# Shared-key attention and a routed expert layer on one core: smaller GpSimd copies, another engine for one DMA, and reordered steps

## The chip, the cores and the metric

The kernel is one program on one core of a Trainium2 chip. The metric is device time in microseconds (us). Three runs of the kernel before gave a median of 484.14 us (478.88 to 484.38). One more execution was profiled: 479.42 us by the same measure, 477.7 us of it the profiler's span. TensorE (PE) multiplies, ScalarE (ACT) applies functions, VectorE (DVE) does elementwise work and reductions, GpSimd (POOL) does copies and the indirect DMAs, and SyncE (SP) only issues DMAs.

## What is computed

The input `x` holds 8 batches of 256 rows with 256 columns, 2048 tokens. Cut to what matters, the reference is

```
xn  = layernorm(x)                                   # over 256 columns
q   = xn Wq' + bq ; k, v = xn Wk' + bk, xn Wv' + bv  # 16 heads of 16; ONE key and value head
s   = q k' / 4, causal ; attn = softmax(s)
att = (attn v) Wout' + bout
top = the 4 largest of softmax(xn Wr') over 16 experts, scaled to sum 1
ffn = sum over the 4 chosen e of top_e * ((silu(xn Wg_e) * (xn Wu_e)) Wd_e)
out = x + att + ffn
```

All arithmetic is fp32. Queries and keys are held as a high part and a remainder, stacked along the contracted partitions, so that one matmul in the fp32r type gives full scores.

## The kernel before, in words

Every engine runs its own instruction list, in the order in which the functions are called in its block. Semaphores join them. The program has three stages.

**Front.** The tokens are worked in four groups of 512 (`g` = 0 to 3). DVE measures mean and variance and forms the scale (`measure`, `scale`, lines 1099 to 1119), ACT writes the normalised rows (`normalise`, line 906), PE transposes them (line 617) and projects to keys, values and router logits (line 647) and queries (line 659), ACT and DVE split each into high part (lines 946, 958) and remainder (lines 1193, 1208). SP stores queries and keys to DRAM (`q_d`, `k_d`, lines 371, 367) and loads them back in the layout that the scores want: keys by `load_k` (line 346), queries by `load_q` (line 351, 8 DMAs per batch, into one of three buffers `qs`). POOL fills constant rows. Partitions 64 to 95 of `qs` hold rows that say which query of a block of 32 a column is; `from_rows(buf)` (line 463) writes them. Together with constant rows of the keys `ks` they add the causal mask inside the matmul.

**Batches.** For each batch there are 12 blocks of scores (`NB`). A block is computed twice. The first pass, `scores_for_max` (line 638), contracts 96 rows, and DVE takes the maximum of each block in `row_max` (line 1188), which allows PE at most two blocks ahead. When the 12 blocks of a batch are done, DVE joins the maxima (`join_max`, line 1278), PE transposes them (`transpose_max`, line 687), and DVE forms the negative maximum of each query as a high part and a remainder (`split_max`, lines 1284 to 1287, semaphore `nm_ready`). Two DMAs write these as rows 96 and 97 of `qs` (`load_m`, line 387, semaphore `m_in`). The second pass, `scores` (line 696), contracts 98 rows, so that ACT can apply the exponential directly (line 979). The first pass runs 18 blocks ahead of the second. In step `s` of batch `b`, PE computes one block of each pass, and then what the step number calls for: the product with the values (`weigh_v`, line 707), the transpose of the context (`context`, line 719), of the divided context (`transpose_context`, line 729) and the output projection (`project_out`, line 735). ACT copies between these (`keep_context`, line 985; `keep_cxt`, line 990), DVE divides (`normalise_context`, lines 1292, 1295) and adds (`add_out`, line 1303). `transpose_context` writes the PSUM bank that also holds the transposed maxima, so it waits for `nm_ready`.

The router works in the shadow of the first batches: `top_logits`, `top_experts`, `shift_tops`, `mark_choices` (line 1165, a one-hot table), `join_choices` (line 1172), `sum_tops`. From batch 2, step 9 on, 16 calls of `list_rows` on PE (line 743), one every second step, collect the token list of each expert tile from tables that POOL (line 543) and DVE (line 1310) write.

**Experts.** 79 tiles of 128 rows: POOL gathers rows with one indirect DMA (line 557), PE, ACT and DVE compute the expert, and POOL adds the result to DRAM with another (line 571).

What the change touches on each engine: on SP the loop over `g` and the calls `load_k(GW, T)` and `load_m(0)` behind it; on POOL `from_rows`, the key copies `copy_k(b)` (line 483, from the loaded keys to `ks`), the additions of the output bias `add_bias(g)` (line 474) and `weigh_choices` (line 512); on PE and ACT one step number each in `batch`; on DVE the front's loop over `g`, and in `batch` the places of `split_max`, `normalise_context` and the router's first marks.

## Time and profile before

| | |
|---|---|
| three runs | 484.14, 478.88, 484.38 us |
| profiled execution | 479.42 us, span 477.7 us |
| PE matmul busy | 410.7 us, 86% of the span |
| POOL busy | 297.5 us, 62% |
| DVE busy | 209.4 us, 44% |
| ACT busy | 187.3 us, 39% |
| front | 0 to 65 us |
| batches | 65 to 191 us |
| experts | 191 us to the end |

Busy shares of a whole span are means over three stages with different limits. What a step costs is read from the stage in which it lies: from the timelines of two engines side by side, where one shows an idle gap ("[1.65 <-ACT early L906]": idle 1.65 us until that instruction of ACT ended), and from the chain of work that ended last.

### The profile page before, as it was taken

To read this page: it belongs to the slowest core of one execution; us is meant where nothing else is said; L and a number is where in the kernel's file an instruction comes from. 1 tells how busy PE (TensorE), PEld (TensorE's weight loads), DVE (VectorE), ACT (ScalarE), POOL (GpSimd) and SP (SyncE) were. 2 spreads that over 40 slices of the span, in tenths; PEclk is the share of its full clock that TensorE was granted. 3 is DMA by queue.
4 is the path that set the end of the run, shared out by engine and by line. 5 is a ranking of instruction groups with operands and counts; after the bars stand their busy time and mean duration, and the time that the engine had idled before them with its cause. 6 is when DMAs were issued, how large, how long until landed. Compare 5 with 4: busy or idle time off the path is not lost.

```text
span 477.7 us, 6790 instructions
## 1 busy us (share of the span) xinstructions
PE 410.7 (86%) x1687; PEld 226.5 (47%) x1688; DVE 209.4 (44%) x514; ACT 187.3 (39%) x439; POOL 297.5 (62%) x304
## 2 busy tenths in 40 slices
PE   3998779788989797889999999999999999999920
PEld 1342334445545343456655555555555555545510
DVE  5778877887886652122223223322222322323300
ACT  4483134456675555323333323333333333323300
POOL 7955331059992021148788788788788788888740
PEclk9998658999999999899999999999999999999985
DMA  7289935987699456525455545445444544446126
GB/s 240 89 204 240 263 106 134 192 176 132 169 251 162 136 150 208 165 60 88 71 82 88 75 72 87 71 82 83 73 79 81 80 79 82 79 73 84 24 36 140
DMA packets 54034, 57.17 MB, mean 120 GB/s; under 512 B 11376, under 2 KB 48928, under 8 KB 53760
## 3 DMA queue, kind: packets, MB, share of 16 engines
q0 software_dynamic: 15440, 21.51, 27.4%
q1 hardware_dynamic: 25904, 22.87, 21.1%
q10 hardware_dynamic: 12672, 12.58, 8.9%
q8 instruction: 7, 0.11, 0.1%
q14 instruction: 11, 0.09, 0.1%
HBM read 37.40 MB, written 23.33 MB: 127 GB/s over the span
## 4 chain that ended last, share of the span: by engine, by line
PE 44%; issue 14%; POOL 11%; DMA 10%; DVE 8%; SPq 5%; ACT 4%; ACTq 0%; POOLq 0%; DVEq 0%
PE bank L830 15%; PE bank L846 8%; POOL late L557 6%; DMA late<-xn_d,get_row 4%; PE bank L707 4%; PE bank L735 3%; PE bank L696 3%; PE bank L638 3%; PE bank L820 3%; POOL out_dram L571 2%; DVE pmax L1188 2%; POOL odd_d L571 2%; SPq L351 2%; PE bank L838 2%; DMA qs_wgu<-nm 1%
## 5 line engine op out<-in xcount | busy, mean ns | idle before, releaser
L830 PE MATMUL bank<-wgu,late 128*128 x316 | 151.6, 602 | 3.0 <-issue 1.2
L557 POOL DMA_INDIRECT late<-xn_d,get_row x79 | 83.5, 1056 | 72.3 <-PE bank L696 28.7
L1399 DVE SCALAR_TENSOR_TENSOR late<-late,bank 128x256 f32<-128x256 f32 x79 | 37.9, 480 | 156.7 <-ACT late L1055 156.7
L846 PE MATMUL bank<-wdn,late 128*128 x316 | 81.5, 380 | 1.4 <-DVE late L1406 1.4
L1055 ACT ACTIVATE late<-bank 128x256 f32<-128x256 f32 x79 | 30.4, 385 | 129.7 <-PE bank L830 129.7
L979 ACT ACTIVATE pt<-bank 128x512 f32<-128x512 f32 x96 | 56.0, 599 | 62.8 <-PE bank L696 61.7
L1188 DVE TRANSPOSE_TENSOR_REDUCE pmax<-bank 128x16 f32<-128x512 f32 x96 | 66.3, 705 | 24.8 <-PE bank L638 24.3
L830 PEld LDWEIGHTS bank<-wgu,late 128*128 128x128 f32 x316 | 53.7, 190 | 46.1 <-issue 45.4
L571 POOL DMA_INDIRECT out_dram<-late,slots x40 | 63.6, 1589 | 19.0 <-issue 9.5
L571 POOL DMA_INDIRECT odd_d<-late,slots x39 | 61.9, 1588 | 12.8 <-issue 9.8
L846 PEld LDWEIGHTS bank<-wdn,late 128*128 128x128 f32 x316 | 53.9, 190 | 6.5 <-issue 2.4
L1406 DVE COPY late<-bank 128x256 f32<-128x256 f32 x79 | 33.5, 424 | 32.4 <-PE bank L838 32.3
L820 PEld LDWEIGHTS bank<-ident,late 128*128 128x128 f32 x158 | 19.5, 140 | 56.2 <-DMA late<-xn_d,get_row 44.2
L1066 ACT ACTIVATE late<-bank 128x256 f32<-128x256 f32 x79 | 30.4, 384 | 39.2 <-PE bank L846 39.2
L543 POOL TENSOR_SCALAR wgu<-iota_p,slot_pf 128x128 f16<-128x128 f32 x64 | 38.7, 625 | 0.3
L820 PE MATMUL bank<-ident,late 128*128 128x128 f32 x158 | 31.7, 282 | 6.1 <-DMA late<-xn_d,get_row 5.8
L638 PE MATMUL bank<-qs_late,ks 96*128 96x512 f32 x60 | 31.9, 542 | 4.5 <-DVE pmax L1188 4.3
L1059 ACT ACTIVATE late<-bank 128x256 f32<-128x256 f32 x79 | 30.0, 380 | 6.9 <-PE bank L820 6.6
L838 PE MATMUL bank<-ident,late 128*128 128x128 f32 x158 | 30.2, 273 | 0.0
L707 PE MATMUL bank<-pt,v_all 128*32 128x512 f32 x192 | 27.3, 642 | 0.0
L838 PEld LDWEIGHTS bank<-ident,late 128*128 128x128 f32 x158 | 22.2, 141 | 7.9
L483 POOL CAST ks<-wdn 64x640 fp32r<-64x640 f32 (+1 forms) x16 | 11.0, 713 | 23.7 <-PE bank L696 16.0
(143 smaller groups left out, 402.2 us busy)
## 6 DMA issues: line engine op xcount, KB each, us to landing
qs_late<-q_d SPq DMA_DIRECT2D x40, 128.0 KB, 4.7
q_d<-early SPq DMA_DIRECT2D x16, 256.0 KB, 4.6
wgu<-in_L_ffn_w_gate_dram ACTq DMA_DIRECT2D x8, 512.0 KB, 5.2
wgu<-in_L_ffn_w_up_dram ACTq DMA_DIRECT2D x8, 512.0 KB, 4.6
wdn<-in_L_ffn_w_down_dram ACTq DMA_DIRECT2D x8, 512.0 KB, 4.3
qs_wgu<-q_d SPq DMA_DIRECT2D x24, 128.0 KB, 4.5
xs<-in_L_attn_x_dram SPq DMA_DIRECT2D x4, 512.0 KB, 4.0
xn_d<-early SPq DMA_DIRECT2D x4, 512.0 KB, 4.3
```

What stands on the lines that cost most here:

```text
L543: pool.tensor_scalar(hot_p[:, t % HOTS, c], iota_p[:], slot_pf[:, t, c:c + 1], None, ALU.is_equal).then_inc(hot_p_ready, 1)
L557: pool.indirect_dma_start(xg[:, j % RING, :], None, xn_d, bass.IndirectOffsetOnAxis(ap=get_row[:, j:j + 1], axis=0), bounds_check=last_row ...
L571: pool.indirect_dma_start(odd_d if j % 2 else out_rows, bass.IndirectOffsetOnAxis(ap=slots[:, j:j + 1], axis=0), ys[:, j % RING, :], None, ...
L638: pe.matmul(bank[:, N % 2, :], k, q, start=True, stop=True).then_inc(p1_ps, 1)
L707: mm = pe.matmul(bank[32 * j:32 * j + 32, 5, :], v_all[:, 2 * b + kt, :], weights[:, j], start=(kt == 0), stop=(g != 1), skip_group_check= ...
L820: t = pe.transpose(bank[:, 7, c * P:(c + 1) * P], xg[:, r, c * P:(c + 1) * P], ident[:, :])
L830: mm = pe.matmul(bank[:, 2 + buf, :], xT[:, buf, c, :], wgu[:, bass.ds(e * KC + c, 1), :], start=(c == 0), stop=(c == KC - 1))
L838: t = pe.transpose(bank[:, 6, c * P:(c + 1) * P], hh[:, buf, c * P:(c + 1) * P], ident[:, :])
L846: mm = pe.matmul(bank[:, 4 + buf, 0:D], hT[:, buf, c, :], wdn[:, bass.ds(e * FC + c, 1), :], start=(c == 0), stop=(c == FC - 1))
L979: act.activation(pt[:, G % 2, n % NU, :], bank[:, 3 + N % 2, :], ACT.Exp).then_inc(exp_done, 1)
L1188: dve.tensor_reduce(found, bank[:, N % 2, :].rearrange("p (h q) -> p h q", h=H), AX.X, ALU.max, apply_transpose=True).then_inc(max_done, 1)
L1399: dve.scalar_tensor_tensor(out=hh[:, buf, :], in0=hh[:, buf, :], scalar=xg[:, r, bass.ds(e + D, 1)], in1=bank[:, 2 + buf, F:2 * F], op0=AL ...
```

## The change

Nothing of the arithmetic is changed. The parts are:

1. `from_rows` writes each half of a buffer in four copies of 512 elements, not in one of 2048. The counts in the waits on `qs_padded` follow.
2. On ACT, behind the copy of the output weights, two DMAs write the first batch's maxima. SP's `load_m(0)` is gone.
3. Keys are loaded in three parts: a second part (`load_k(GW, 2 * GW)`) stands in SP's loop at `g == 2`, the rest comes where it came before. `copy_k(2)` and `copy_k(3)` wait for the second part only. POOL does all `add_bias` and `copy_k(2)` ahead of `weigh_choices(0)`.
4. `mark_choices(0)` and `join_choices(0)` move from DVE's front loop to steps 4 and 5 of batch 0. `split_max(0)` moves ahead of `sum_tops(0)`.
5. In each batch, `context(b - 1, 1)` on PE moves from step 3 to step 4, behind `project_out(b - 1, 0)`. `normalise_context(b - 1, 1)` on DVE moves from step 5 to step 6, and `keep_cxt(b - 1, 1)` on ACT from step 10 to step 9.
6. `split_max(b + 1)` moves within DVE's step 8 ahead of the step's `row_max`.

```diff
@@ SP @@
                 if g == 0:
                     load_k(0, GW)
+                if g == 2:
+                    load_k(GW, 2 * GW)
                 if g < 3:
...
-            load_k(GW, T)
+            load_k(2 * GW, T)
 
             for g in range(2, NG):
                 sp.wait_ge(q_stored[g], 64)
-            load_m(0)
@@ POOL @@
             def from_rows(buf):
                 for half in range(2):
-                    pool.tensor_copy(qs[buf][64:96, half].rearrange("p h (u q) -> p (h u) q", q=QC),
-                                     from_q[64:96].unsqueeze(1).to_broadcast([32, H * NU, QC])).then_inc(qs_padded, 1)
+                    for h in range(0, H, H // 4):
+                        pool.tensor_copy(qs[buf][64:96, half, h:h + H // 4].rearrange("p h (u q) -> p (h u) q", q=QC),
+                                         from_q[64:96].unsqueeze(1).to_broadcast([32, H // 4 * NU, QC])).then_inc(qs_padded, 1)
...
-                pool.wait_ge(k_all_in, 64 if b < 2 else 128)
+                pool.wait_ge(k_all_in, 64 if b < 2 else 128 if b < 4 else 192)
...
             shift_logits(0)
-            add_bias(1)
-            weigh_choices(0)
-            for g in range(2, NG):
+            for g in range(1, NG):
                 add_bias(g)
-            pool.wait_ge(coef_ready, 1)
             pool.wait_ge(xb_ready, NT)
             copy_k(2)
             pool.wait_ge(k_ready, 6)
+            weigh_choices(0)
             shift_logits(1)
@@ PE, batch @@
                         if s == 3:
+                            project_out(b - 1, 0)
+                        if s == 4:
                             context(b - 1, 1)
-                            project_out(b - 1, 0)
@@ ACT @@
             act.activation(woT[:].rearrange("p c e -> p (c e)"), bank[:, 6, :], ACT.Copy).then_inc(w_act, 1)
+            act.wait_ge(nm_ready, 1)
+            for a in range(2):
+                act.dma_start(qs[0][96 + a:97 + a].rearrange("o e h t -> o (e h t)").bitcast(F32),
+                              nm[:, a, :].bitcast(F32)).then_inc(m_in[0], 16)
...
-                        if s == 10:
+                        if s == 9:
                             keep_cxt(b - 1, 1)
@@ DVE @@
                 if g == 2:
-                    mark_choices(0)
-                    join_choices(0)
                     row_max(0, 0)
...
+                if (b, s) == (0, 4):
+                    mark_choices(0)
+                if (b, s) == (0, 5):
+                    join_choices(0)
...
+                    if s == 8 and b < B - 1:
+                        split_max(b + 1)
                     n = b * NB + s + NB + NB // 2
                     if n < B * NB:
                         row_max(n // NB, n % NB)
...
-                        if s == 5:
+                        if s == 6:
                             normalise_context(b - 1, 1)
...
-                    if s == 8 and b < B - 1:
-                        split_max(b + 1)
...
             join_max(0)
+            split_max(0)
             sum_tops(0)
-            split_max(0)
```

How DVE's order moves in the front, from the third group's query remainders on. Before (`chosen` and `wgu` are the router's tables, `pmax` the block maxima):

```order
L1208 SCALAR_TENSOR_TENSOR early<-bank,bq_s,early 128x512 x2
L1165 TENSOR_TENSOR wgu<-top_ef,iota_e 128x512
L1172 TENSOR_REDUCE chosen<-wgu 128x128
L1188 TENSOR_REDUCE pmax<-bank 128x16
L1193 SCALAR_TENSOR_TENSOR early<-bank,bvrk,early 16x512
```

and now:

```order
L1213 SCALAR_TENSOR_TENSOR early<-bank,bq_s,early 128x512 x2
L1193 TENSOR_REDUCE pmax<-bank 128x16
L1198 SCALAR_TENSOR_TENSOR early<-bank,bvrk,early 16x512
L1193 TENSOR_REDUCE pmax<-bank 128x16
L1213 SCALAR_TENSOR_TENSOR early<-bank,bq_s,early 128x512
```

The two router instructions no longer stand ahead of the first block maximum; they come in batch 0.

How PE's order moves in steps 3 and 4 of a batch (here batch 1). Before, step 3 begins at the first row:

```order
L638 MATMUL bank<-qs_late,ks 128x512
L696 MATMUL bank<-qs_late,ks 128x512
L719 MATMUL bank<-ident,ct 128x128 x4
L735 MATMUL bank<-woT,out_buf 128x256 x2
L638 MATMUL bank<-qs_late,ks 128x512
L696 MATMUL bank<-qs_late,ks 128x512
```

and now:

```order
L638 MATMUL bank<-qs_late,ks 128x512
L696 MATMUL bank<-qs_late,ks 128x512
L735 MATMUL bank<-woT,out_buf 128x256 x2
L638 MATMUL bank<-qs_late,ks 128x512
L696 MATMUL bank<-qs_late,ks 128x512
L719 MATMUL bank<-ident,ct 128x128 x4
```

The context transpose, which waits for ACT's copy `ct`, comes one projection and one pair of score blocks later.

SP's issues of groups 2 and 3, before:

```order
L371 DMA q_d<-early 128x4x128 x4
L351 DMA qs_late<-q_d 16x2x1024 x8
L367 DMA k_d<-early 16x512 x2
L371 DMA q_d<-early 128x4x128 x4
L346 DMA wdn<-k_d 16x1536 x4
L387 DMA qs_wgu<-nm 1x128x32 x2
```

and now:

```order
L371 DMA q_d<-early 128x4x128 x4
L346 DMA wdn<-k_d 16x512 x4
L351 DMA qs_late<-q_d 16x2x1024 x8
L367 DMA k_d<-early 16x512 x2
L371 DMA q_d<-early 128x4x128 x4
L346 DMA wdn<-k_d 16x1024 x4
```

Four issues more stand in this run, and the first maxima are no longer at its end.

## Rows read from the trace of the kernel before

**Rows 1.** The page: PE's granted clock in tenths, in 40 slices of 11.94 us.
```profile
PEclk9998658999999999899999999999999999999985
```

**Rows 2.** Busy time by stretch: us, PE (x) PEld (x) DVE (x) ACT (x) POOL (x), clock, DMA share, GB/s.
```profile
131.00:147.00 16.00, 14.26 (x93) 8.38 (x93) 13.00 (x29) 10.66 (x23) 15.16 (x24) 1.00 0.96 231
...
265.00:340.00 75.00, 72.48 (x277) 42.36 (x276) 20.81 (x46) 24.66 (x69) 60.94 (x47) 1.00 0.48 79
```

**Rows 3.** DVE's timeline, front: start, duration, engine, line, operation, [idle before <-releaser].
```profile
18.64 1.52 DVE L1114 TENSOR_TENSOR rstd<-rstd,var_e 128x4 f32<-128x4 f32 x1
...
22.39 1.58 DVE L1118 SCALAR_TENSOR_TENSOR shift<-mv,rstd 128x4 f32<-128x4 f32 x1
...
29.09 0.16 DVE L1114 TENSOR_TENSOR rstd<-rstd,var_e 128x4 f32<-128x4 f32 x1
```

**Rows 4.** POOL's timeline, front: a copy of 512 elements, and the copies of 2048.
```profile
14.20 0.61 POOL L456 CAST ks<-after_q 32x512 fp32r<-32x512 f32 x1
...
16.42 3.72 POOL L463 CAST qs_wgu<-from_q 32x2048 fp32r<-32x2048 f32 x2
```

**Rows 5.** Timelines of ACT and PE, front, third group.
```profile
24.00 2.08 ACT L906 ACTIVATE early<-xs,shift,rstd 128x256 f32<-128x256 f32 x4 [2.26 <-DVE shift L1118]
...
24.66 1.92 PE L617 MATMUL bank<-ident,early 128*128 128x128 f32 x8 [1.65 <-ACT early L906]
```

**Rows 6.** DVE's timeline, front, around the first block maximum.
```profile
40.05 0.75 DVE L1165 TENSOR_TENSOR wgu<-top_ef,iota_e 128x512 bf16<-128x512 f32 x1
40.83 1.04 DVE L1172 TENSOR_REDUCE chosen<-wgu 128x128 bf16<-128x512 bf16 x1
41.79 0.71 DVE L1188 TRANSPOSE_TENSOR_REDUCE pmax<-bank 128x16 f32<-128x512 f32 x1
```

**Rows 7.** PE's timeline, front, last group's query projections.
```profile
39.55 1.95 PE L659 MATMUL bank<-early,wqT 128*128 128x512 f32 x4
42.55 0.50 PE L638 MATMUL bank<-qs_wgu,ks 96*128 96x512 f32 x1 [1.04 <-DVE pmax L1188]
...
44.42 3.42 PE L659 MATMUL bank<-early,wqT 128*128 128x512 f32 x4
```

**Rows 8.** The chain that ended last, 56 to 65 us: start, duration, what.
```profile
56.56 5.17 DMA q_d<-early
...
62.80 2.15 DMA qs_wgu<-nm
```

**Rows 9.** Timelines of DVE and PE: first maxima, first block of the second pass.
```profile
56.99 0.66 DVE L1287 TENSOR_TENSOR nm<-nm_f,nm 128x32 fp32r<-128x32 f32 x1
...
61.69 0.76 PE L638 MATMUL bank<-qs_late,ks 96*128 96x512 f32 x1 [0.36 <-DVE pmax L1188]
64.99 0.80 PE L696 MATMUL bank<-qs_wgu,ks 98*128 98x512 f32 x1 [2.53 <-DMA qs_wgu<-nm]
```

**Rows 10.** SP's timeline: the four loads of the last keys.
```profile
59.15 1.71 SPq L346 DMA_DIRECT2D wdn<-k_d  x4
```

**Rows 11.** The chain that ended last, later: the slowest transfer of maxima.
```profile
158.04 4.86 DMA qs_wgu<-nm
```

**Rows 12.** Waits of PE, 82 to 195 us: total us, times, longest us.
```profile
PE bank L719 <- ACT ct L985: 4.7, 7, 1.0
PE bank L735 <- ACT out_buf L990: 3.9, 8, 0.7
PE bank L729 <- issue: 3.2, 5, 1.3
```

**Rows 13.** DVE's timeline, batch 4: after step 3's wait, and the maxima's last instruction.
```profile
136.16 0.72 DVE L1188 TRANSPOSE_TENSOR_REDUCE pmax<-bank 128x16 f32<-128x512 f32 x1 [1.46 <-PE bank L638]
...
141.81 0.32 DVE L1287 TENSOR_TENSOR nm<-nm_f,nm 128x32 fp32r<-128x32 f32 x1
```

**Rows 14.** Timelines of POOL and PE: list tables, and a list matmul.
```profile
132.51 12.22 POOL L543 TENSOR_SCALAR wgu<-iota_p,slot_pf 128x128 f16<-128x128 f32 x20
...
149.75 0.32 PE L743 MATMUL bank<-wgu 128*128 128x80 f16 x4
```

More of the change, by code:

```diff
@@ L462, in from_rows @@
                 for half in range(2):
-                    pool.tensor_copy(qs[buf][64:96, half].rearrange("p h (u q) -> p (h u) q", q=QC),
-                                     from_q[64:96].unsqueeze(1).to_broadcast([32, H * NU, QC])).then_inc(qs_padded, 1)
+                    for h in range(0, H, H // 4):
+                        pool.tensor_copy(qs[buf][64:96, half, h:h + H // 4].rearrange("p h (u q) -> p (h u) q", q=QC),
+                                         from_q[64:96].unsqueeze(1).to_broadcast([32, H // 4 * NU, QC])).then_inc(qs_padded, 1)
             from_rows(0)
-            pool.wait_ge(qs_padded, 2)
+            pool.wait_ge(qs_padded, 8)
             def add_bias(g):
@@ L486, in _ @@
             from_rows(1)
-            pool.wait_ge(qs_padded, 4)
+            pool.wait_ge(qs_padded, 16)
             add_bias(0)
@@ L492, in _ @@
             from_rows(2)
-            pool.wait_ge(qs_padded, 6)
+            pool.wait_ge(qs_padded, 24)
             copy_k(1)
@@ L633, in scores_for_max @@
                     pe.wait_ge(q_in[b % 3][n // NU], 64 * (b // 3 + 1))
-                    pe.wait_ge(qs_padded, 2 * (b % 3) + n // NU + 1)
+                    pe.wait_ge(qs_padded, 8 * (b % 3) + 4 * (n // NU) + 4)
                 if N >= 2:
```

## The prediction

> **What bounds the kernel now.** I read three views in this order: busy time by stretch, the chain of waits that ended last, and the timelines of PE, DVE, ACT, POOL and SP side by side where the chain changes engine. The first tells the stages apart. In the expert stage PE is busy 72.48 of 75 us with POOL at 60.94 [rows 2]. The change touches nothing there, so I leave that stage, more than half of the span, as it is. In a middle batch (16 us) PE is busy 14.26 us and DVE 13.00 [rows 2]: neither is full, they hand blocks back and forth, and each batch loses time in named gaps. In the front the chain runs through DVE, ACT and PE to the fourth group, then through SP's issues and a DMA to the first block of the second pass.
>
> **The front.** (a) *Quarter copies.* DVE's `scale(2)` has two instructions of 1.52 and 1.58 us at 18.64 and 22.39; the same first one in the next group takes 0.16 [rows 3]. POOL's copies of 2048 elements, 1.86 us each, run back to back from 16.42 and go on for a second buffer [rows 4], and the slow instructions end when a copy ends: 16.42 + 3.72 = 20.14 against 18.64 + 1.52 = 20.16. So DVE waits there for a whole copy, three times (a third, between these two, is of their length). A copy of 512 takes 0.61 us [rows 4], so a wait is at most that and about 0.4 on average: three waits cost 1.2 us, not the roughly 4.3 of now. `scale(2)` ends some 3.2 us earlier, near 20.7. But ACT has other work until 21.75 (24.00 less its idle 2.26), so ACT gains 2.25, and PE, which was idle 1.65 for the first row tile and then followed ACT tile by tile [rows 5], gains about 2.2. Everything behind it in groups 1 and 2 is a chain of ACT, PE and DVE without slack and moves by 2.2. POOL pays four starts for one: 4 x 0.61 = 2.44 against 1.86, 0.6 for each half and 3.5 for six. It has that time, since it sits idle for keys around 27 to 32 us and again for 13 us later.
>
> The Trainium skill (SBUF — State Buffer, section "Who interferes with whom") says that a DVE instruction with two inputs in SBUF and a GpSimd instruction that reads SBUF exclude each other for a whole instruction, the first to issue going first. The trace agrees in the 1.52 us of [rows 3]. If POOL, always first, kept DVE out for a whole run of quarters, DVE would wait for 16 x 0.61 = 9.8 us from 16.42, to 26.2, and lose 2 us where I count 3.2 gained; I take the other reading because DVE's instructions got in between two copies (the slow one above ended with the second copy, and others followed before the third ended).
>
> (b) *Router marks.* DVE did the one-hot and its sum, 0.75 and 1.04 us, right ahead of the first `row_max` [rows 6], for which PE stood idle 1.04 [rows 7]. Without them that maximum is 1.8 us earlier still, but the next one waits for ACT's keys, so the fourth group gains about 1.4 more, 3.6 in all. There is a second effect. PE's projection of the last half took 3.42 us where the same four matmuls took 1.95 before it [rows 7]: the granted clock had gone to 1.2 GHz after two idle gaps. With one of them gone and the other at 0.7 I expect it to still be at 2.4 GHz there, 1.5 us more: 5.1. Bounds: 3.6 and 5.1. Then eight `row_max` follow at DVE's pace, unchanged, so the first maxima, ready at 57.65 now [rows 9], are ready near 52.6. In batch 0 the marks cost DVE 1.8 us again, between steps 4 and 6, where it sits idle about 2 us for PE: nothing. Swapping `split_max(0)` and `sum_tops(0)` (0.4 us) is no gain, since the sums stood in the shadow of a transpose; it pushes the six maxima of batch 1 back by 0.4.
>
> (c) *The first maxima's DMA.* It now leaves behind the last query store, which landed at 61.73, and itself takes 2.15 from its second issue at 62.80 [rows 8]. PE could have begun batch 0 at about 62.2 but waited until 64.99 [rows 9]. Issued by ACT, which has nothing queued behind it before batch 0 needs these rows, it leaves at 52.7, with the second issue at 53.3. It then runs beside SP's transfers. Its duration is not in the trace for this place: 2.15 is the quiet value [rows 8], 4.86 the one with a crowd of other transfers [rows 11]. I take 4.5, as the queues are full there: 57.8. PE's side is ready at 62.2 - 5.1 + 0.4 = 57.5. So batch 0 begins near 57.9, **7.1 us earlier**. With a low clock in (b) it is 58.9 and 6.1; with a DMA of 2.15 nothing is added, since PE is the later one.
>
> The Trainium skill (DMA: Bandwidth & Descriptors, section "Queues, rings and completion order") says that each DMA engine takes turns between the queues it has work for. By that the maxima would not stand behind SP's backlog and would need nearer 2.15 than 4.86. The sum would gain only 0.3.
>
> (d) *Keys in three parts.* Four more issues on SP, 4 x 0.43 = 1.7 us [rows 10], stand ahead of the queries of batch 2 and of the last stores. SP is continuously busy there from 24.66 on; it now starts 3.2 earlier with (a), so the last query store lands 1.5 earlier, not later, and nobody waits for it but the first expert load. `copy_k(2)` was ready at 64.7 for a use at 72; now it is ready near 52. Worth nothing by itself, but needed: its slack of 7 us would be what (c) takes.
>
> **The batches.** Between 82 and 195 us PE waits 4.7 us in seven places for the copy `ct` ahead of `context(b-1, 1)`, 3.9 in eight for the copy ahead of `project_out`, and 3.2 in five ahead of `transpose_context(b-1, 1)`, which is held by `nm_ready` [rows 12].
> - The first goes: with the projection and a pair of blocks (0.9 + 0.6 us) ahead of it, `ct` is long there. 4.7.
> - The second: `keep_cxt` at step 9 follows its transpose at once, no longer behind an exponential. Seven of the eight are this one: 3.4.
> - The third: DVE's chain in batch 4 from 136.16, after 1.46 us idle, to 142.13 is nearly unbroken [rows 13]. Its start moves with PE's block of step 4, which comes 1.0 earlier (0.5 of wait and 0.5 of transposes go behind it), and `split_max` no longer has a `row_max` of 0.65 ahead of it. PE's wait of 0.54 goes. 3.2 in all.
>
> Together 11.3. What is late next is the maxima's DMA: in batches 5 and 6 PE already waits for it at the start of the next batch, with 4.86 us [rows 11], and there only the earlier `nm_ready` counts, 1.1 and 0.7. That leaves 0.9 of the 11.3 on the path: **10.4**. Batch 0 to 1, where PE waits for the same DMA, gains 0.65 from `split_max`: **0.7**.
>
> Not covered: POOL. It writes list tables without a pause, 0.61 us each, 20 in 12.22 us [rows 14]; the last of 64 is ready at 144.7 and used at 149.75 [rows 14]. That lead of 5.0 us shrinks by the 4.5 that three batches gain; the tables behind a `copy_k` have 4.0. I take 0.6 back.
>
> Sum: 7.1 + 0.7 + 10.4 - 0.6 = 17.6. Against the profiled execution, 479.42 - 17.6 = **461.8**. That execution is 4.7 below the median of the three runs and 0.5 above the lowest; the same gain from 484.14 gives 466.5. I give 464 for a median of runs that may fall at either.
>
> **The rivals.**
> 1. *Only the front gains.* DVE and PE are coupled over two blocks; `row_max` of step 8 now follows `split_max`, and DVE, busy 13 of 16 us, may hand back at steps 9 to 11 what was won. For: both engines are above 80%. Against: after step 9 DVE shows idle gaps of about 1 us for PE. Gain 7.8, time 471.6 to 476.3.
> 2. *Only the batches gain,* because the front ends in something else (the port, the DMA of maxima, the queries of batch 1 from a full SP). With 2 to 4 of the 7.1 left: gain 12.5 to 14, time 465 to 471.
> 3. *The clock, slower.* The clock is low from about 45 to 75 us [rows 1] and costs little, as DVE sets the pace. If DVE's added 1.8 us in batch 0 and the shifted handoffs leave PE too broken up, it stays low in batches 1 to 5. Four matmuls take 3.42 for 1.95 then [rows 7], so 14.26 us of PE work would be some 22 to 24 in a batch of 16: 6 to 8 us lost for each. It decides from the fourth such batch: 462 + 4 x 7 = 490, and to 500. Against: with the gaps shorter, PE is busier.
> 4. *Nothing.* Both parts turn into waits of the same size: 479 to 484.
>
> **How the numbers follow.** Forecast 0.66, rival 1 0.13, rival 2 0.14, rival 3 0.02, rival 4 0.05. From 484.14, 2% is 9.7 us, about what a measurement of this kernel can tell from no change: 474.5. The forecast and rival 2 are faster (0.80), with a third of rival 1 (0.04); the rest of rival 1 (0.09) and rival 4 (0.05) are within 2% (0.14); rival 3 is slower (0.02). The range: the forecast's bounds are 461.8 less 2 where parts add (a quick DMA, a batch 0 at 2.4 GHz) and less 2 for a low run, 458, and 466.5 with a low clock in (b) and twice the loss to POOL, 469. To take in rival 2 and the lower half of rival 1 it reaches to 474.5.
>
> **What the next profile would show.** Right: DVE's instructions of `scale(2)` under 0.8 us; PE's second projection of group 3 near 1.95 us; the first second-pass block near 58 us; no wait of PE for `ct`; batches of about 14.6 us, not 16.2; tiles as before. Wrong: the projection at 3.4 us; PE waiting for a `row_max` at steps 9 to 11 by 0.5 us or more a batch; list matmuls waiting for POOL by over 1 us in all; a maxima DMA of over 6 us.

## The result, and the profile after

The changed kernel took 468.09 us (median of four runs, 464.84 to 472.9) against 482.29 us (478.88 to 484.38) before: ratio 0.9701, interval 0.9648 to 0.9755. Timed again (the last run below) it gave 0.9694 (0.9638 to 0.9750). The forecast's range of 458 to 474.5 holds the median, which lies 4 us above the 464. The ratios leave out executions more than 1.5% above the fastest of their kernel, such as the 472.9 here and the profiled 470.96 of the last run below. The gain of 14.2 us between medians is less than the 17.6 us that the prediction summed, and between the two profiled executions it is 9.4: 479.42 to 470.03, span 477.7 to 468.3.

Where did it come from? Busy time by stretch shows it (us, PE (x) PEld (x) DVE (x) ACT (x) POOL (x), granted clock, DMA share, GB/s). The cuts are the first block of the second pass and the first expert matmul. Before:

```profile
0.00:65.00 65.00, 46.23 (x127) 19.73 (x128) 47.90 (x139) 27.54 (x55) 40.59 (x68) 0.87 0.78 202
65.00:196.07 131.07, 112.99 (x606) 60.11 (x606) 89.31 (x214) 73.91 (x147) 51.55 (x81) 0.95 0.72 173
...
```

After:

```profile
0.00:61.87 61.87, 45.11 (x127) 19.07 (x128) 44.96 (x137) 27.55 (x55) 42.34 (x86) 0.87 0.85 201
61.87:186.97 125.10, 112.26 (x605) 60.56 (x606) 91.37 (x216) 74.63 (x147) 51.36 (x81) 0.94 0.77 182
...
```

The front gives 3.1 us where 7.1 were forecast, the batches 6.0 where 10.5 were (0.7 + 10.4 - 0.6), and the rest of the span 0.3 (281.6 to 281.3). The engines' busy times in the whole span are nearly the same (PE 410.7 and 410.5 us); what went is waiting.

**The batches.** The waits of PE from 60 to 190 us (line, who released it: total us, times, longest us) answer to [rows 12]:

```profile
PE bank L696 <- DMA qs_late<-nm: 5.2, 3, 2.0
PE bank L696 <- DMA qs_wgu<-nm: 4.1, 2, 2.8
PE bank L638 <- DVE pmax L1193: 1.6, 5, 0.3
...
PE bank L719 <- DVE out_buf L1298: 0.7, 1, 0.7
PE bank L729 <- issue: 0.7, 1, 0.7
...
PE bank L735 <- ACT out_buf L995: 0.5, 1, 0.5
```

The three waits that the change aims at summed to 11.8 and sum to 1.9. In their place stand the first two lines: PE waits for the DMA that brings the next batch's maxima. Less the 2.8 at batch 0 it is 6.6 us, at the start of batches 2, 5, 6 and 7. The DMAs did take longer (min/median/max from issue to landing of all of SP's `load_m`, in the kernel before with batch 0's among them), before and then after:

```profile
DMA to landing us min/median/max: 2.0/2.8/4.9
```

```profile
DMA to landing us min/median/max: 2.0/4.3/5.5
```

**The front.** DVE's timeline answers to [rows 3], the chain of waits to [rows 8], with ACT, PE and POOL around the fourth group between them (start, duration, line, operation, [idle before <-releaser]):

```profile
19.21 0.54 DVE L1119 TENSOR_TENSOR rstd<-rstd,var_e 128x4 f32<-128x4 f32 x1
19.79 0.52 DVE L1120 TENSOR_TENSOR rstd<-rstd,std 128x4 f32<-128x4 f32 x1
20.34 0.54 DVE L1121 TENSOR_SCALAR rstd<-rstd 128x4 f32<-128x4 f32 x1
```

```profile
30.73 1.26 POOL L485 CAST ks<-wdn 64x640 fp32r<-64x640 f32 x2 [2.44 <-DMA wdn<-k_d]
32.06 4.51 POOL L465 CAST qs_late<-from_q 32x512 fp32r<-32x512 f32 x8
36.64 1.27 POOL L485 CAST ks<-wdn 64x640 fp32r<-64x640 f32 x2
37.99 0.41 POOL L507 TENSOR_TENSOR logits<-logits,top_w 128x128 f32<-128x128 f32 x1
```

```profile
38.43 0.31 ACT L918 ACTIVATE probs<-logits 128x128 f32<-128x128 f32 x1 [1.17 <-POOL logits L507]
```

```profile
41.59 0.50 PE L638 MATMUL bank<-qs_wgu,ks 96*128 96x512 f32 x1 [1.78 <-DVE pmax L1193]
41.93 2.76 PE L659 MATMUL bank<-early,wqT 128*128 128x512 f32 x4
```

```profile
53.80 0.20 DVE nm L1290
...
54.02 0.55 ACTq L976
...
54.62 7.21 DMA qs_wgu<-nm
...
61.87 0.80 PE bank L696
```

The quarters did what was expected of them: the three slow instructions of `scale(2)` take 0.54 us or less each. Then POOL is late. Its copies for buffer 2 take 4.51 us for 3.73, they stand between two key copies and the shift of the router's logits, and the keys came late, at 30.7 us, where most runs below with the same front have them at 29.0 to 29.6.

That lateness begins at 12 us, in the second group's `scale`. DVE's third instruction there took 1.15 us and ended with a constant fill on POOL (12.36 + 1.05 = 13.41). In e5 below it took 0.17:

```profile
12.29 1.15 DVE L1121 TENSOR_SCALAR rstd<-rstd 128x4 f32<-128x4 f32 x1
```

```profile
12.36 1.05 POOL L459 MEMSET ks<- 32x1152 f32 x1
```

```profile
12.30 0.17 DVE L1121 TENSOR_SCALAR rstd<-rstd 128x4 f32<-128x4 f32 x1
```

The long form is in five of the fourteen profiled executions: this one, e7, e8, e11 and e12. In these, DVE begins the third group's `scale` at 19.2 us and not at 18.3 to 18.6. In four of them, all but e7 with its whole copies, SP stores the third group's queries from 22.2 and POOL waits 1.9 to 2.5 us for the keys; the other executions with quarters have 21.0 to 21.6 and 0.6 to 1.3. No part of the change touches this place. So a time in the front is best compared between executions that begin alike.

Back at the fourth group, ACT waits 1.17 us for the logits, PE 1.78 for a maximum, and the last projection takes 2.76 us, part of it at 1.2 GHz. The maxima are ready at 54.0, not near 52.6, and their DMA takes 7.2 us, not 4.5.

### The profile page after: what moved, and what is told of

The parts are those of the page before. It is cut to its first block, busy times and chain, and to the rows that moved or that the text cites. A ratio compares the mean times of both kernels' runs of the same rounds, so it can differ in the third digit from the quotient of the medians.

```text
span 468.3 us, 6811 instructions
## 1 busy us (share of the span) xinstructions
PE 410.5 (88%) x1687; PEld 226.4 (48%) x1688; DVE 208.6 (45%) x514; ACT 187.9 (40%) x439; POOL 298.9 (64%) x322
## 4 chain that ended last, share of the span: by engine, by line
PE 37%; issue 18%; POOL 18%; DMA 11%; DVE 8%; ACT 3%; SPq 2%; ACTq 0%; POOLq 0%; DVEq 0%
PE bank L831 11%; POOL late L557 10%; PE bank L847 5%; PE bank L707 5%; PE bank L638 4%; PE bank L696 4%; POOL odd_d L571 4%; DVE pmax L1193 3%; DMA qs_late<-nm 3%; POOL out_dram L571 3%; DMA qs_wgu<-nm 3%; DMA late<-xn_d,get_row 2%; PE bank L735 2%; PE bank L821 2%; DMA out_dram<-late,slots 1%
## 5 line engine op out<-in xcount | busy, mean ns | idle before, releaser
L821 PEld LDWEIGHTS bank<-ident,late 128*128 128x128 f32 x158 | 19.2, 140 | 54.2 <-DMA late<-xn_d,get_row 43.1
L696 PE MATMUL bank<-qs_late,ks 98*128 98x512 f32 x60 | 24.8, 425 | 5.7 <-DMA qs_late<-nm 5.2
L485 POOL CAST ks<-wdn 64x640 fp32r<-64x640 f32 (+1 forms) x16 | 10.4, 675 | 25.0 <-PE bank L696 14.8
```

The source lines that it names most:

```text
L696: pe.matmul(bank[:, 3 + N % 2, :], k, q, start=True, stop=True).then_inc(s_ps, 1)
L821: t = pe.transpose(bank[:, 7, c * P:(c + 1) * P], xg[:, r, c * P:(c + 1) * P], ident[:, :])
```

## The experiments

"Batch 0" is the start of the first block of the second pass, "the stretch" the time from there to the first expert matmul: 64.99 and 131.08 before, 61.87 and 125.10 after.

**e1_front_only: parts 1 to 4.** The edit takes parts 5 and 6 back:

```diff
                         if s == 3:
+                            context(b - 1, 1)
                             project_out(b - 1, 0)
-                        if s == 4:
-                            context(b - 1, 1)
```

(and likewise for `keep_cxt`, `normalise_context`, `split_max`.)

> Parts 1 to 4 of the change alone (quarter copies, first maxima's DMA on ACT, keys in three parts, router marks in batch 0); the batches' step numbers and the place of split_max as before. Theory A (the transfers of a batch are what bounds it after the change, so the two halves of the change do not add in full): batch 0 begins near 61.9 us as in the changed kernel, 3.1 earlier than before, and the stretch from there to the first expert matmul takes 130 to 131 us as before (64.99 to 196.07), since batches of 16.2 us leave the DMA engines time to drain. Span about 474.5, ratio near 0.994. Theory B (the front's gain is partly lost in the batches by DVE's two marks): that stretch is longer, 132 to 133 us, and nothing or 1 us is left of the gain.

Measured: 473.18 us, ratio 0.9843 (0.9753 to 0.9933). Batch 0 at 58.91, the stretch 131.08, as before to the hundredth. PE's waits in the batches are back, and those for the maxima are short:

```profile
PE bank L719 <- ACT ct L989: 4.7, 7, 1.0
PE bank L729 <- issue: 3.2, 5, 1.3
PE bank L735 <- ACT out_buf L994: 2.7, 6, 0.7
...
PE bank L696 <- DMA qs_late<-nm: 1.4, 2, 1.1
```

The front alone gives 6.1 us at batch 0 and keeps it. It is the same front as in the changed kernel, whose batch 0 began at 61.87 in its profile. Here DVE's early instruction was short, the keys were in time, ACT waited 0.47 us for the logits and the projection took 1.88.

**e2_batches_only: parts 5 and 6.** The kernel before with those edits.

> Parts 5 and 6 alone (context to step 4, normalise to step 6, keep_cxt to step 9, split_max ahead of row_max). Theory A: batch 0 begins at 65.0 us as before; PE's waits ahead of L719, L729 and L735 between batches 1 and 7 fall by about 10 us, and 4 to 5 us come back as waits for the maxima's DMA, so the stretch to the first expert matmul is 125 to 126 us instead of 131.1. Gain 5 to 6, ratio near 0.988. Theory B (the batches' lost gain comes of the shifted front, by another phase of the transfers): the stretch is 121 us, gain 10, ratio 0.979.

Measured: 473.75 us, ratio 0.9826 (0.9720 to 0.9932). Batch 0 at 66.03, the stretch 124.96. So the batches' parts give 6.1 us by themselves, with the old front: what is missing of the forecast 10.5 is lost inside the batches and needs no new front. The product of the two ratios is 0.967, that of the whole change 0.970: within the intervals the halves add. Each alone is a gain of under 2%, but both intervals end below 1.

**e3_first_m_on_sp: the first maxima's DMA back on SP,** behind the last query stores.

```diff
-            act.wait_ge(nm_ready, 1)
-            for a in range(2):
-                act.dma_start(qs[0][96 + a:97 + a]...
...
                 sp.wait_ge(q_stored[g], 64)
+            load_m(0)
```

> The changed kernel with the first maxima's DMA again on SP, behind the last query stores and the third part of the keys. Theory A (the 7.2 us of this DMA on ACT are SP's backlog on the 16 DMA engines, and it would be served no sooner from SP): SP issues it at about 64 us, it lands in 2.2 us in empty queues, PE begins batch 0 near 67 us, 5 us later than with ACT; of these 5, 0 to 4 come back later, as the span is bounded by transfers in the batches. Theory B (a DMA from ACT is slow by itself, as the first of its queue): from SP it takes 2.2 us all the same; this run alone does not part the two, the next one does.

Measured: 479.39 us (one run). The chain of waits:

```profile
55.42 6.65 DMA q_d<-early
62.15 0.57 SPq L389
...
62.76 2.18 DMA qs_wgu<-nm
...
64.98 0.79 PE bank L697
```

The maxima were ready near 51.2 and stood for 11 us behind the stores. Batch 0 begins at 64.98, where it began before. All else that the front gains arrives only through this one move. The batches gained nothing here either: the stretch is 131.04, with parts 5 and 6 in place. PE waits 9.9 us in it for maxima, 5.25 of them at batch 2, where one DMA took 8.4 us and the granted clock fell to 1.2 GHz (0.50 from 100 to 106 us). Why that batch met so much isn't known, so the whole 11 us between this run and the others are not the price of the move.

**e4_keys_in_two: part 3's extra load undone,** to see whether the four key issues on SP make the maxima's DMA slow.

```diff
-                if g == 2:
-                    load_k(GW, 2 * GW)
...
-            load_k(2 * GW, T)
+            load_k(GW, T)
```

> The changed kernel without the second part of the keys in SP's loop (keys in two parts, as before); all else as changed. SP spent 4.5 us on these four issues at 46.15 us. Theory A (backlog): the queries of batch 2 and the last stores leave 3 to 4.5 us earlier, the backlog that the first maxima meet at 54.6 us is shorter by as much, the DMA lands in 3 to 4 us instead of 7.2, and PE begins batch 0 near 59 us, where its own six blocks end. Theory B (slow by itself, as the first DMA of ACT's queue): it still takes about 7 us, batch 0 begins near 61.9. In both copy_k(2) ends near 62, before its use in step 6.

Measured: 465.37 us (one run), batch 0 at 58.35, the DMA 5.6 to 6.1 us. That misses the 3 to 4 expected of fewer issues: SP's eight query loads then took 6.38 us to issue for 3.68 and SP came out only about 1 us earlier than in the changed kernel. So this run doesn't tell bytes from issues; e9 does.

**e5_stores_late and e6_stores_weights_late: less for the maxima to meet in the batches.** The first issues two stores (logits, 128 KB, and zeros, 2 MB) in batch 5; the second also shifts four loads of expert weights.

```diff
-                if b == 0:
+                if b == 5:
                     sp.wait_ge(coef_ready, 2)
...
-                if b == 3:
+                if b == 5:
                     zeros = zero_t[:].rearrange("p t e -> p (t e)")
@@ e6 only @@
-                    if b == 5 and s in (7, 9):
-                        load_experts(4, s // 9)
+                    if b == 5 and s in (10, 11):
+                        load_experts(4, s - 10)
...
-                    if b == B - 2 and s in (5, 7):
-                        load_experts(B - 2 + s // 7, 2)
+                    if b == B - 2 and s in (9, 11):
+                        load_experts(B - 2 + s // 11, 2)
```

> The changed kernel with two SP transfers moved out of the batches that are full: the store of the routing weights (128 KB in 64-byte pieces, 10.7 us to landing in batch 1) and the 2 MB of zeros (14 us, batch 4) both go behind the maxima of batch 6, where no more queries are loaded. Theory A (a batch's transfers must drain before its maxima's DMA can land, and shorter batches ran into that): PE's waits for the maxima at the start of batches 2 and 5 (1.7 and 2.1 us) go to under 0.5, those at batches 6 and 7 (1.4, 1.5) stay or grow by 1 as the zeros now pass there; batches 0 to 5 take 76 us and not 79.3. Theory B (the maxima's DMA is slowed by the query loads and weights alone): the two waits stay above 1.2.

Measured: 469.92 us (one run), batch 0 at 57.89, the stretch 129.2. The wait at batch 5 went, with the zeros. But batch 2 waited 3.26 us though the logits' store was gone, and batch 7 3.50, behind zeros that now leave at 150 us. The granted clock fell behind both waits (0.78 from 94 to 100 us, 0.65 from 166 to 174). The stretch is 4.1 us longer than the changed kernel's, where less was expected.

> As the last, and the expert weights that were issued right ahead of the maxima in batches 5 and 6 (steps 7, 9 and 5, 7) go behind them (steps 10, 11 and 9, 11). Theory A: the waits at batches 6 and 7 fall to under 0.7 as well; from batch 0 to the first expert matmul 120 to 121 us, not 125.1, which is the 10.4 us that the prediction summed for the batches. Span 4 us under the changed kernel's at equal front, ratio to the kernel before 0.962 to 0.966. Theory B: 124 us or more, or the first expert matmul waits for the last weights.

Measured: 462.12 us (460.6 to 469.5), ratio 0.9598 (0.9505 to 0.9692). The stretch is 120.03, a gain of 11.0 where the prediction had 10.5. Waits of PE from 60 to 182 us, and the maxima's DMAs:

```profile
PE bank L696 <- DMA qs_late<-nm: 3.3, 3, 2.1
...
PE bank L719 <- DVE out_buf L1298: 0.7, 1, 0.7
PE bank L729 <- issue: 0.7, 1, 0.7
...
PE bank L696 <- DMA qs_wgu<-nm: 0.2, 1, 0.2
```

```profile
DMA to landing us min/median/max: 2.1/2.9/3.7
```

The forecast size of the batches' gain is there, and the maxima's DMAs are back at 2.9 us in the median. The median alone doesn't carry it, though: it is 2.7 in e5 and 3.1 in e2, with stretches of 129.2 and 124.96. What differs is the sum of PE's waits for maxima behind batch 0 (3.4 us here, 8.0 in e5, 4.4 in e2) and the clock, which here is 1.00 from 82 us to the end of the stretch. e5 and e6 run the same program up to batch 5 and yet their waits at batch 2 are 3.26 and 0.21 us: what a DMA of maxima meets varies between executions. And from batch 5 on e6 needs 43.9 us, as e7, e8 and e9 do with the stores in their old places (44.2, 43.9, 43.5): what e6 has over e7 and e8 lies in batches 0 to 4, and there it runs the same program as e5, which needs 3.8 us more. How much of e6's gain is owed to the moved transfers isn't settled.

**e7_whole_copies: part 1 undone.**

```diff
-                    for h in range(0, H, H // 4):
-                        pool.tensor_copy(qs[buf][64:96, half, h:h + H // 4]...
+                    pool.tensor_copy(qs[buf][64:96, half].rearrange("p h (u q) -> p (h u) q", q=QC),
```

> The changed kernel with the constant rows again in copies of 2048 elements. If the prediction's first step is right, two or three of DVE's instructions of the scale wait 1.5 us or more again, the fourth group's first block maximum comes 1.5 to 2.5 us later than in the changed kernel (38.1 us), and SP's first query store too (24 to 25 us, not 22.2). Batch 0 then begins 1.5 to 2.5 us later than with quarters in an execution whose last projection runs at the same clock (58.9 at 2.4 GHz, 61.9 at 1.2), so at 60.5 to 64. If the copies did not matter: no difference in either.

Measured: 467.99 us (one run), batch 0 at 62.11. DVE's timeline, as [rows 3]:

```profile
19.21 0.94 DVE L1118 TENSOR_TENSOR rstd<-rstd,var_e 128x4 f32<-128x4 f32 x1
...
20.38 1.80 DVE L1120 TENSOR_SCALAR rstd<-rstd 128x4 f32<-128x4 f32 x1
...
22.43 1.57 DVE L1122 SCALAR_TENSOR_TENSOR shift<-mv,rstd 128x4 f32<-128x4 f32 x1
```

The changed kernel's profile is the run to set beside it, since DVE begins `scale(2)` at 19.21 in both. `scale(2)` ends at 24.00 and not at 21.54, and PE begins the third group's query projection at 26.45 and not at 23.98: 2.5 us, where the prediction said 2.2. More followed from it. PE, idle 2.07 us before the third group, took 5.29 us for eight matmuls that take 3.60 there:

```profile
24.70 1.92 PE L616 MATMUL bank<-ident,early 128*128 128x128 f32 x8 [2.07 <-ACT early L906]
26.45 5.29 PE L658 MATMUL bank<-early,wqT 128*128 128x512 f32 x8
```

The fourth group's first block maximum comes 3.1 us later (41.25 for 38.11). The first maxima are ready only 1.2 us later (55.2 for 54.0), and batch 0 begins 0.2 later, because the changed kernel's last projection ran partly at 1.2 GHz and this one took 1.88. So the copies' 2.5 us are shown in the third group, and not at batch 0.

**e8_marks_front: the router's marks back ahead of the first `row_max`.**

```diff
                 if g == 2:
+                    mark_choices(0)
+                    join_choices(0)
                     row_max(0, 0)
```

> The changed kernel with the router's two marks again in the front, ahead of the first block maximum. If the prediction's second step is right: that maximum is at 40 us, PE waits for it by 0.7 to 1.1 us and once more for the next, and the last projection takes 2.7 to 3.4 us (it took 1.88 in three of four executions with the marks moved, 2.76 in one). The first maxima are ready 1 to 3 us later than the 51.5 of those three, and batch 0 begins at 60 to 62. Rival: the next block maximum waits for ACT's keys anyway, so the marks cost nothing, the projection takes 1.88 and batch 0 begins at 59.

Measured: 467.39 us (one run), batch 0 at 62.04, the maxima issued at 54.3, 2.9 later than e5's. But this is an execution with DVE's long instruction at 12.3 us, and e5 is not. e11 below is one too, and its DVE reaches the place of the marks at the same time (36.35 there, 36.33 here) with no marks in it. Against e11 the first block maximum is done 1.7 us later (40.10 for 38.39), the second 0.6 later (41.62 for 41.02), since in e11 DVE stands idle 1.14 us for ACT's keys between the two, and the first maxima are ready 2.5 later (54.3 for 51.8). The last projection took 3.01 us, not 1.88: 1.1 of the 2.5 is its clock. Against e12, where the logits are late, the second maximum is no later at all (41.62 for 41.61). So the marks cost 0 to 0.6 us here, and 1.1 by the clock behind them.

**e9_queries_later: the bytes ahead of the first maxima.** SP loads the third batch's queries only once the first maxima are ready.

```diff
-                    if g == 0 or g == 2:
+                    if g == 0:
                         sp.wait_ge(q_stored[g // 2], 64)
-                    for half in range(2):
-                        load_q(g, half)
+                    if g < 2:
+                        for half in range(2):
+                            load_q(g, half)
...
                 sp.wait_ge(q_stored[g], 64)
+            sp.wait_ge(nm_ready, 1)
+            for half in range(2):
+                load_q(2, half)
```

> The changed kernel, but SP loads the third batch's queries (8 DMAs of 128 KB, 8 us of transfer) only once the first maxima are ready, behind the last query stores; ScalarE still issues those maxima. Theory A (backlog): the maxima's DMA took 5 to 7 us in the front because the DMA engines had the bytes of these queries in hand. Without them it lands 2.2 to 4 us behind its second issue, PE is then the later one, and batch 0 begins 0.5 to 1.5 us earlier than in the run with the late stores (57.9), near 57. The queries are first needed near 66 us by PE's first pass, and land near 61 to 63: no wait. Whole time 1 us less than with them early, 464 to 468. Theory B (the issuing queue: a DMA from ScalarE into these rows is slow by itself): it still takes 5 us or more, and nothing moves. Theory C: PE's first pass of batch 2 waits for the late queries, or the second batch's maxima are now late instead; batch 1 or 2 loses 1 to 3 us.

Measured: 464.45 us (one run), batch 0 at 55.73. DMAs issued from 50 to 62 us (KB each, median us to landing), here and then in e10, which has the queries in their old place:

```profile
qs_wgu<-nm ACTq DMA_DIRECT2D x2, 16.0 KB, 2.4
```

```profile
qs_wgu<-nm ACTq DMA_DIRECT2D x2, 16.0 KB, 6.2
```

That is backlog, shown: the same two DMAs from the same engine take 2.4 us instead of 6.2 once 1 MB of query loads stands behind them, and PE no longer waits for them. Theory C holds too. PE waits 1.28 us for the late queries, and 2.09 at batch 1 for that batch's maxima, whose DMA takes 5.56. Batch 1 begins at 74.42, against 73.45 in e5, though batch 0 began 2.2 earlier: the backlog only moved by one batch.

**e10_split_behind_max: part 6 alone undone.**

```diff
-                    if s == 8 and b < B - 1:
-                        split_max(b + 1)
                     n = b * NB + s + NB + NB // 2
...
+                    if s == 8 and b < B - 1:
+                        split_max(b + 1)
```

> The changed kernel, but DVE's split_max of the next batch stands again at the end of step 8, behind that step's row_max. This takes back part 6 alone. Theory A (the prediction's third term): PE's waits ahead of transpose_context(b-1, 1) come back in part, 0.3 to 0.6 us in four or five batches, and the maxima's DMAs leave 0.7 us later, which lengthens the waits for them in batches 2, 5, 6 and 7 (6.6 us in sum now) by 0.5 each; whole time 2.5 to 4.5 us more than the changed kernel. Rival B: the transposes at step 9 are late enough by themselves since other waits went, and only the maxima's waits grow: 1 to 2 us. Rival C: row_max of step 8 comes 1.1 us earlier for PE, which pays back what the maxima lose: no difference over 1 us.

Measured: 467.61 us (one run), batch 0 at 58.66, the stretch 125.93, 0.8 more than with part 6. The transposes' wait is back:

```profile
PE bank L729 <- issue: 3.4, 5, 1.3
```

It was 0.7 with part 6. So part 6 removes 2.7 us of one wait, as Theory A has it, but the time is that of rival C: the batches are 0.8 us longer without it, and executions with the same batches differ by more (125.1 in the changed kernel, 122.9 and 122.2 in e7 and e8). The maxima's waits in the batches are 6.6 us with and without it. What part 6 is worth in time stays open, between nothing and these 2.7 us.

**e11_all_late: e6, e4 and e9 together.**

> All that the runs pointed to, together: the two stores and the expert weights issued later (which gave 462.12 us, ratio 0.9598), keys in two parts, and the third batch's queries issued behind the first maxima. Theory A (these add, since each is about what stands in the DMA engines when a maxima's DMA leaves): batch 0 begins near 57, stretch of the batches 120 us, time 459 to 462, ratio 0.953 to 0.960. Rival B: with the stores gone the backlog at the first maxima is all that is left and PE is already the later one there, so nothing is added: 461 to 463. Rival C: copy_k(2) gets its keys later again and the queries of batch 2 come late, so batch 0 or 1 loses 1 to 3 us: 463 to 466.

Measured: 461.68 us (461.04 to 462.86), ratio 0.9624 (0.9562 to 0.9687), the same as e6. Batch 0 begins at 56.72, the stretch is 121.57. The 0.9 us won at the start went in batch 1. Rival C had named a loss there, but by late keys and queries; this one has another cause. PE's timeline:

```profile
81.96 0.63 PE L721 MATMUL bank<-ident,ct 128*128 128x128 f32 x4 [0.74 <-DVE out_buf L1300]
82.49 0.50 PE L640 MATMUL bank<-qs_wgu,ks 96*128 96x512 f32 x1
82.83 0.40 PE L698 MATMUL bank<-qs_late,ks 98*128 98x512 f32 x1
83.94 0.66 PE L731 MATMUL bank<-ident,out_buf 128*128 128x128 f32 x2 [0.71 <-issue]
84.53 1.94 PE L709 MATMUL bank<-pt,v_all 128*32 128x512 f32 x8
```

After two idle gaps of 0.7 us the granted clock fell to 1.2 GHz (0.63 in the mean from 82 to 88 us), and eight matmuls took 1.94 us. The same eight behind the same two gaps took 1.06 in e6, and batch 1 15.6 us there against 17.9 here.

**e12_changed_again: the changed kernel, timed again.**

> The changed kernel once more, nothing edited, in five rounds. Two questions. Where does batch 0 begin in another execution? Theory A: at 57.6 to 58.9, as in the five runs that share its front, with PE's second projection near 1.9 us and no wait of ScalarE over 0.5 us for POOL's logits; 61.87 was one execution in which the keys' loads came late. Rival B: near 62 again, so the late logits belong to this kernel, and the later stores of other variants cured them. Is it slower than the kernels with the later stores and weights (0.960 and 0.962 of the kernel before)? Theory A: ratio 0.968 to 0.974, its batches 124 to 127 us against 120 to 122, and the two to five us lie in waits for the maxima's DMAs. Rival B: ratio 0.960 to 0.965, and those kernels gained nothing.

Measured: 468.37 us (463.3 to 470.96), ratio 0.9694 (0.9638 to 0.9750). Batch 0 at 59.96, between the two answers: POOL waited 2.52 us for the keys and ACT 1.25 for the logits, as in the first profile, but the projection took 1.88, with PE idle 1.79 before it. DVE's instruction at 12.3 us took 1.15 here too. So late logits belong to this kernel in the executions that begin so, and a low clock behind them in some of those. Against e6 and e11 theory A fits, with ratios of 0.969 and 0.970 on one side and 0.960 and 0.962 on the other, but the intervals overlap: that these two are the better kernels is likely, and not shown.

## Why the prediction was right, point by point

**Right, and why.** The forecast rested on two independent gains, and each came alone: 6.1 us from the front (e1) and 6.1 from the batches (e2). Rival 1 falls with that, and so does rival 4. Rival 3 falls in its size, but not in its kind: the granted clock is 1.00 from 76 us on but for one fall (0.80 from 142 to 150 us), of which more below. (By its own factor, 3.42 for 1.95, its 22 to 24 us for a batch should have been 25.) Rival 2 had a part of it: in the profiled execution the front does end in the DMA of maxima and gives 3.1 us, within its 2 to 4. But e1 and e5 show 6.1 and 7.1 from the same front and e12 5.0, so 3.1 is one execution's price, and rival 2 had the batches give all they were forecast, which they did not.

**(a) Quarter copies, 2.2 us.** Right: 2.5 by e7 at the third group's query projection, and no instruction of `scale(2)` over 0.54 us. The reading that DVE gets in between two quarters holds: three instructions took 0.54, 0.52 and 0.54 us while POOL ran sixteen quarters in a row. By the Trainium skill (SBUF — State Buffer, section "Who interferes with whom") the first to issue holds the port for one instruction; the trace agrees, and DVE did not have to wait for the end of POOL's run.

"POOL has that time" was wrong in the profiled execution. POOL's idle time lies ahead of the key copies, and the added 0.8 us for buffer 2 lies behind them, on the way to the router's logits, for which ACT now arrives 2 us earlier. ACT's wait was 1.17 us, of which the longer copies are 0.8 at most; the late keys are the rest. With the clock behind it the maxima were ready at 54.0, and in e1 and e5 at 51.4 and 51.3. That step was not in the sum. Nor was another, of the other sign: ahead of the first maxima DVE's last two instructions took 0.43 and 0.66 us before, while POOL ran additions from 56.20 on, and 0.18 and 0.19 now that part 3 has moved those forward. That is 0.7 us, and part of why the maxima of e1 and e5 come 6.3 us earlier where 5.1 were summed.

**(b) Marks, 1.4 us and 1.5 of clock.** The clock's part was right in kind: the projection took 3.01 us with the marks (e8), and with this front 1.88 in nine executions and 2.76 in the first profiled one; that is 1.1 of the 1.5. The marks' own part was 0.6 by e11 and nothing by e12, since the next block maximum waited for ACT's keys. No run has the marks in an execution with early keys, so the 1.4 stays open there. In batch 0 the marks cost nothing: it took 15.7 us, 16.1 before.

**(c) The first maxima's DMA, 4.5 us.** The step was right in kind, as e3 shows, and its term mis-sized: 5.4 to 7.2 us from the second issue with the queries in flight. The bound of 4.86 was taken from a batch with a DMA share of 0.45 (158 to 163 us); here the share is 1.08 (54.6 to 61.8). In the executions where the maxima were early (issued at 51.4 to 51.6) this ate what (a) and (b) had won beyond the forecast, and batch 0 began at 57.6 to 58.9, beside the forecast 57.9. With the late logits it was 61.87 and 59.96. By the Trainium skill (DMA: Bandwidth & Descriptors, section "Queues, rings and completion order") the engines take turns between queues, so that ACT's DMA would have needed nearer 2.15. No run agrees while the queries are in flight (5.4 to 7.2); without them it took 2.4 (e9) and 4.0 (e11).

**(d) Keys in three parts, nothing.** Nearly right: `copy_k(2)` ran at 54.1, not 52, and without the early part nothing was lost (e4). The issues took 4.50 us, not 1.7. SP's third group began 2.4 us earlier, as (a) has it for ACT, and not 3.2, and the last query stores were issued from 55.37, 0.4 later than before and not 1.5 earlier.

**The batches, 10.4 us.** The waits went nearly as forecast: the three lines fell by 9.9 us, 11.8 to 1.9, where 11.3 was summed. The step that failed is "what is late next": the prediction kept 0.9 us on the path for the maxima's DMA, with its duration as before. The waits for it behind batch 0 grew from 1.9 to 6.6 us, by 4.7, where the sum had 0.9 more and, at batch 1, 0.7 less. These 4.5 us are the size of what is missing between 10.5 and 6.0. The 1.4 that the three lines fell short is about made up by the 0.6 of the lists and by PE's waits for block maxima (2.8 to 1.6 us). Why the DMAs are late is in part argued: a shorter batch has to move the same bytes, the DMA share rose from 0.72 to 0.77 and the median landing from 2.8 to 4.3 us, and e9 shows the backlog for one batch; but e6, which moves bytes away, differs from e5 by 3.8 us where the two run the same program.

Waits are not all of it. e7 and e8 run the changed kernel's batches, PE waits 6.2 and 5.4 us there for maxima, and their stretches are 122.9 and 122.2 us, gains of 8.2 and 8.9 where the changed kernel's profile has 6.0. The clock goes with the difference, here in the changed kernel and then in e7:

```profile
142.00:150.00 8.00, 8.00 (x45) 4.14 (x45) 3.91 (x7) 4.54 (x9) 0.59 (x2) 0.80 0.71 128
```

```profile
142.00:150.00 8.00, 8.00 (x48) 4.46 (x45) 5.23 (x11) 5.56 (x12) 0.21 (x1) 1.00 0.81 124
```

Both waited 2.0 us for maxima at 141 us; in one the clock fell, in the other it didn't. Before, in e7 and in e8 it is 1.00 from 82 to 180 us; in e2 it falls twice (0.76 from 94 to 100, 0.67 from 142 to 150). So the new waits cost more than their own length in some executions. That is rival 3's mechanism in small, by these stretches 2 to 3 us for one fall, and no run parts it from the waits.

**The lists, -0.6.** Not seen: no wait for the tables appears in the waits after.

**The total.** 464 came nearer than its profiled terms because the median of before lay above its profiled execution, while that of after lay below. The size of each half was forecast as 7 and 10.5 and came as 6 and 6 in e1 and e2; in the changed kernel's first profile the front gave 3.1 of it. That 464 lies so near is in part luck of this kind; that both halves gain is not.

## What to carry to other kernels

Before a part is priced by taking it back, see that the two executions begin alike: here one DVE instruction at 12 us, 1 us longer in five of fourteen executions, moved the front by 0.6 to 1.2 us. When waits are taken out of a loop, price again every transfer that the loop starts: its bytes stay, its time shrinks, and a small DMA that was on time queues behind them. Moving a DMA to an idle engine's queue saves the issue order, not the backlog; for that, bytes must be issued later, and one must look where they then land. A cover named as "the engine is idle there" has to lie behind the added work and ahead of its next reader, not merely near it.

## What was not expected of the hardware

- The four loads of the last keys, 96 KB each, cost SP 1.71 us to issue [rows 10], and four of 32 KB cost 4.50 at 46 us in the changed kernel (3.49 in e1, 5.05 in e5). The DMA share was 1.16 at the quick ones and 1.08 at the slow ones, so full DMA engines alone don't explain it; the cause is open.
- Two idle gaps of 0.7 us were followed by a fall to 1.2 GHz in e11 and not in e6; 1.79 us idle left the projection at 1.88 us in e12, 1.78 at 2.76 in the profiled one. Equal gaps give unequal clocks, and such a step is worth 0.9 to 2.3 us.
- The quarters moved DVE's waits in part: in the next group `scale` now meets POOL's additions, with 0.65 us for instructions that took 0.16:

```profile
26.98 0.65 DVE L1120 TENSOR_TENSOR rstd<-rstd,std 128x4 f32<-128x4 f32 x1
27.67 0.66 DVE L1121 TENSOR_SCALAR rstd<-rstd 128x4 f32<-128x4 f32 x1
```
